# Where VectorE takes the skip and dB in the first two groups with a second phase

## The reference

```python
xz = x @ W_in                                   # 256 -> 2 * 512
x_proj, z = jnp.split(xz, 2, axis=-1)
x_conv = silu(depthwise_conv4(x_proj) + conv_b)  # 4 taps along the sequence
ssm = x_conv @ W_xproj                          # 512 -> 1 + 16 + 16
delta, Bm, Cm = softplus(ssm[..., 0]), ssm[..., 1:17], ssm[..., 17:]
h_mean = einsum('bld,bln->bdn', x_conv, delta[..., None] * Bm) / L
y = einsum('bdn,bln->bld', h_mean, Cm) + D * x_conv
x = layernorm(x + (y * silu(z)) @ W_out)
xq = fp4(x)
h = silu(xq @ fp4(w_gate).T) * (xq @ fp4(w_up).T)
out = layernorm(x + fp4(h) @ fp4(w_down).T)
```

## Time and profile before

| | us |
|---|---|
| median of 3 runs | 1895.02 |
| lowest and highest | 1894.50, 1896.96 |
| the profiled execution | 1894.42 |
| its span | 1892.6 |
| TensorE busy | 1790.6 (95%) |
| VectorE busy | 1625.0 (86%) |
| ScalarE busy | 1269.6 (67%) |
| GpSimd busy | 1120.1 (59%) |

### The profile page before, as it was taken

The page is one execution under the profiler, slowest core; times in us unless marked ns, Lnnn a source line. Parts: engine busy times, 40 slices in busy tenths (PEclk is TensorE's granted clock), DMA queues, the critical chain, the costliest instruction groups (busy, mean ns, idle before and its releaser), DMA issues. The chain is left out here.

```text
span 1892.6 us, 34609 instructions
## 1 busy us (share of the span) xinstructions
PE 1790.6 (95%) x10180; PEld 1545.5 (82%) x10180; DVE 1625.0 (86%) x3697; ACT 1269.6 (67%) x2617; POOL 1120.1 (59%) x1847
## 2 busy tenths in 40 slices
PE   6887999999999999999999999999999999899986
PEld 5666788888888888888888888888888888777775
DVE  6745899899988989999998999899999988888885
ACT  6676677677767777677776777667776776544543
POOL 3334566666656666666666666566666665555453
PEclk9898999999999999999999999999999999999998
DMA  5224232333333233333323333333333333122200
GB/s 175 89 106 159 95 113 94 101 115 114 105 98 109 98 115 104 107 109 108 110 96 106 104 115 104 106 110 97 110 107 106 107 101 106 51 84 68 84 23 17
DMA packets 120312, 190.62 MB, mean 101 GB/s; under 512 B 15040, under 2 KB 49728, under 8 KB 120128
## 3 DMA queue, kind: packets, MB, share of 16 engines
q1 hardware_dynamic: 120128, 188.42, 29.8%
HBM read 104.48 MB, written 83.89 MB: 100 GB/s over the span
## 5 line engine op out<-in xcount | busy, mean ns | idle before, releaser
L572 PE MATMUL pgu<-wgu_hi,xqT 128*128 128x512 f32 (+1 forms) x1536 | 415.2, 379 | 16.6 <-issue 15.4
L572 PEld LDWEIGHTS pgu<-wgu_hi,xqT 128*128 128x128 f32 x1536 | 278.5, 188 | 66.6 <-issue 18.8
L572 PE MATMUL pd<-wd_hi,hqT 128*128 128x256 f32 x1536 | 287.6, 287 | 6.0 <-DVE scratch L1302 2.6
L572 PEld LDWEIGHTS pd<-wd_hi,hqT 128*128 128x128 f32 x1536 | 240.7, 193 | 11.1 <-issue 5.7
L572 PE MATMUL pgu<-wgu_lo,xqT 128*128 128x512 f32 (+1 forms) x768 | 226.6, 376 | 0.0
L1163 DVE SCALAR_TENSOR_TENSOR acc<-xps,cw,acc 128x512 f32<-128x512 f32 x256 | 198.4, 775 | 22.7 <-POOL acc L478 18.0
L1078 DVE SCALAR_TENSOR_TENSOR scratch<-scratch 128x256 f32<-128x256 f32 (+2 forms) x258 | 173.2, 671 | 41.6 <-ACT scratch L957 40.5
L653 PE MATMUL pd<-wout,g 128*128 128x256 f32 x864 | 204.4, 380 | 0.0
L439 POOL TENSOR_SCALAR rs<-ssq 128x1 f32<-128x1 f32 x256 | 79.2, 309 | 201.8 <-issue 187.6
L855 ACT ACTIVATE scratch<-scratch,sum 128x256 f32<-128x256 f32 x256 | 130.0, 508 | 93.3 <-DVE scratch L1248 83.3
L686 PEld LDWEIGHTS pc<-wxp,xcs 128*128 128x128 f32 x1024 | 132.0, 194 | 66.0 <-issue 37.2
(11 more groups left out here) (160 smaller groups left out, 4594.6 us busy)
## 6 DMA issues: line engine op xcount, KB each, us to landing
sz_hbm<-szs SPq DMA_DIRECT2D x128, 256.0 KB, 2.0
xc_hbm<-xcs SPq DMA_DIRECT2D x128, 256.0 KB, 2.0
early<-xc_hbm SPq DMA_DIRECT2D x128, 256.0 KB, 2.7
early<-sz_hbm SPq DMA_DIRECT2D x128, 256.0 KB, 3.0
xin<-in_x_t_dram SPq DMA_DIRECT2D x32, 512.0 KB, 4.7
xres<-in_L_attn_x_dram SPq DMA_DIRECT2D x128, 128.0 KB, 2.4
out_dram<-scratch SPq DMA_DIRECT2D x128, 128.0 KB, 1.7
early<-in_L_attn_W_in_dram SPq DMA_DIRECT2D x2, 512.0 KB, 4.7
```

Source lines behind the costliest of these rows:

```text
L572: mm = pe.matmul(bank, lhsT, rhs, start=(m == 0), stop=(m == len(pairs) - 1))
```

## The change

In groups 5 and 6 alone VectorE's order is changed; nothing is added or removed, and the other engines' orders stay.

- In group 5 (`g_ <= LAG`) `skip()` goes from behind the taps, and in the fourth step from behind two splits of the input, to the front of the step. In its second step dB (`scaled_b()`) goes from behind the rests and codes of the weights to directly behind the taps.
- In group 6 (`g_ == LAG + 1`) `skip()` goes from behind the codes of x, the taps, the rounding and the product of h to the front of the step. From group 7 on it stays where it was.

```diff
                     if g_ <= LAG:
+                        if p2:
+                            skip()
                         tap(1)
                         tap(2)
...
-                        if p2:
-                            skip()
+                        if j == 1 and g_ == LAG:
+                            scaled_b()
                         weight_rests(u)
                         weight_codes(u)
                         if j == 1 and 2 <= g_ < LAG:
                             add_state(g_ - 1)
                         if j == 1 and g_ == LAG:
-                            scaled_b()
                             add_state(g_)
...
                     if exists(tz):
                         ffn_sum()
+                    if g_ == LAG + 1:
+                        skip()
                     if exists(tx):
                         x_codes()
...
-                    if p2:
+                    if p2 and g_ > LAG + 1:
                         skip()
```

## The result

The changed kernel takes 1901.18 us (median of 21 runs, 1897.95 to 1903.23) against 1895.08 (21 runs, 1890.64 to 1898.61): a ratio of 1.0032, with a 95% interval of 1.0026 to 1.0038. It is slower by 6.1 us; the forecast was 7.7 (1902.7, in a range of 1897.5 to 1906.5). The profiled execution took 1901.56, its span is 1899.8, 7.2 longer than before. The page's part 1, to be set beside the earlier trace rows: no engine works appreciably longer, TensorE even 3.3 us less, so the time is idle time.

A forecast was written before the change was run, and what follows sets the result against it. TensorE was taken as the bound, busy 95% of the span. Steps 20 to 25 gave -2.4, steps 26 and 27 +7.7, the clock +2.4: +7.7 us on the 1895.02 median, 1902.7, range 1897.5 to 1906.5.

The forecast's parts named there:

- Step 20: Group 5: y was ready anyway, so skip first puts the taps and the projection behind them 0.7 us later.
- Step 21: Group 5: taps regain 0.6 us beside GpSimd, weight rest goes behind dB; TensorE's partial state starts 0.3 us earlier.
- Step 22: Group 5: the taps wait for y too, so the projection starts at 167.0, not 165.61: 1.4 us later.
- (a): Rival: the 1.2 GHz spells of steps 21 to 24 vanish, step 26 at -6.0, sum +4.1, 1899 us; chance 0.18.
- Step 23: Group 5: the SiLU, no longer the skip, releases the projection; it starts at 173.7 us, +0.5.
- Steps 24 and 25: Group 6: input product +1.0 or -0.4, TensorE's 2.58 us wait for the skip goes; step 26 starts 1.8 to 3.0 earlier.
- Steps 26 and 27: Group 6: skip first makes VectorE wait for y, delaying x's codes and gate product: +4.1 and +3.6, together +7.7 us.
- the 2.4: Clock term: new TensorE pauses around step 27 bring 1.2 GHz spells, costing 0 to 4.8 us; +2.4 taken.
- The steady part: From about 198 us on: TensorE is full, so any delay or gain arriving there remains at the end.
- (b): Rival, faster: the wait for y in steps 26 and 27 is taken up; 1889 to 1893 us, chance 0.05.
- (c): Rival: losses partly absorbed or the clock stays up throughout; 1896 to 1898.8 us, chance 0.12.
- (d): Rival: both new pauses cost a long 1.2 GHz spell; +10.7 us, 1905.7, chance 0.10.

The follow-up runs named there:

- g6_26_27: Skip moved to the front in steps 26 and 27 alone, against the kernel before: 1905.83 us, ratio 1.0054.
- g5_24_25: The changed kernel with the skip back in its old place in steps 26 and 27; against the kernel before: 1894.46 us, ratio 0.9988.
- g6_26: Skip moved to the front in step 26 alone, against the kernel before: 1900.21 us, ratio 1.0028.
- best1: Skip first in steps 23 and 25, dB directly behind the skip in step 21, against the kernel before: 1889.39 us, ratio 0.9967.
- g5_25: Skip first in steps 20 to 23 and 25, dB behind the taps in step 21, against the kernel before: 1892.25 us, ratio 0.9980.
- g5_25_y: Skip first in steps 20 to 23 and 25, dB moved, y before the gate product in 26 and 27; against the kernel before: 1892.96 us, 0.9979.
- s23: Skip moved to the front in step 23 alone, against the kernel before: 1894.93 us, ratio 0.9997.
- g5_only: Group 5 of the change alone (skip first in steps 20 to 23, dB moved), against the kernel before: 1891.76 us, ratio 0.9979.
- warm: Changed kernel plus eight unread filler products before step 27's gate product; against the kernel before: 1899.53 us, ratio 1.0018.
- y_first: Changed kernel with TensorE making y before the gate product in steps 26 and 27; against the kernel before: 1892.84 us, ratio 0.9984.
- y_only: Kernel before with y before the gate product in steps 26 and 27, no skip moved: 1895.37 us, ratio 0.9996 to the kernel before.
- g6_24_25: Skip moved to the front in steps 24 and 25 alone, against the kernel before: 1895.27 us, ratio 1.0003.

## Why the prediction was right

**Steps 20 to 23.** *Step 20* as forecast: the projection at 148.57 against 147.68, less the 0.28 by which y of step 20 was later anyway, +0.6 (forecast +0.7). *Step 21*: partial state at 155.68 against 155.53, so -0.1 (forecast -0.3). Its taps beside GpSimd took 1.57 and not 2.17 us, with the skip put under GpSimd's product; that is the stretch which the walk took away, and the rule of the Trainium skill ("SBUF — State Buffer", section "SBUF: two separate sides") agrees with it. In step 23 the taps took 1.53 against 2.42, but there GpSimd's product had ended at 169.29, before the skip began at 169.56: VectorE had waited 1.18 us for y, which the walk didn't have. The skip took 740 to 749 ns in these places. *Step 22* came out otherwise: the projection at 164.75 and not 167.0, because TensorE ran at full clock there and y was ready 0.28 us after VectorE. That is 0.9 us earlier than before (165.61) where the forecast, and its list of signs, had 1.4 later, and it is a part of rival (a). The wait for y is there, as is a pause of TensorE (1.59 us for the SiLU), but it is small. *Step 23*: 172.47, forecast 173.7.

**Steps 24 and 25.** VectorE waits 3.34 us for y in step 24; the input product of step 25 starts at 185.87 (-0.4; forecast +1.0 or -0.4). That the -0.4 comes out is luck: it stood for no slow stretch in step 24, and there is one (the input product of step 24 takes 1.19 us at its start, as before); TensorE only came in earlier, since step 23 was 0.7 early and not 0.5 late. The wait for the skip in step 25 is gone, and step 26 begins at 197.38, that is -1.9 (forecast -1.8 to -3.0). In the trace this term was well sized, in the runs it is less clear: the changed kernel less g6_26_27 gives 6.1 - 10.2 = -4.1, group 5 alone is -4.0, and g5_24_25, which is the change up to step 25 and nothing else, is -2.3, while I had taken -2.4. The intervals are 2 us and more to each side, so whether the 1.6 us between the forecast of +7.7 and the +6.1 lie in this term can't be decided. What it left out is clear from the traces below: it kept the clock in group 5 at 1.2 GHz from 157 to 162 us as before; I had put the other case apart as rival (a), all or nothing, at -6.0.

**Steps 26 and 27.** +4.4 (forecast +4.1) and +5.9, of which 3.6 and part of the 2.4 were forecast. Here all pieces are in the trace: skip behind y, codes at 203.76, gate product released by the rests, 3.79 us of pause (forecast 3.5), 209 to 216 us at 1.2 GHz, 2.68 before the projection (forecast 2.8). Alone they cost 10.2 us; the terms of the sum give 10.1. The clock's share can be read from the rows: from the gate product of step 27 to its y 7.34 us against 5.88 before, from the z product to the down projection (L572 into pd) 2.29 against 1.47, together 2.3. The 2.4 was the middle between 0 and 4.8, so that it fits so well is in part luck.

**The steady part.** 8.40 us late at step 28 and 8.19 at step 33: it absorbs nothing. Further on the distance moves by about 0.6 us with single slow stretches, as said above.

**Rivals.** (b), faster, fell with the wait of 3.79 and with g6_26. (c) fell too: nothing was absorbed and slow stretches came; its own sum doesn't hold together either, since 5.3 us with no slow stretch would be 1900.3 and not 1896 to 1898.8. (d) was not reached: of the two new pauses one had a stretch of 6.8 us with it, the other one of 3.4. (a) was half right: the stretch behind step 21 went, but the changed kernel has three of 3.4 us, from about 165, 175 and 185 us.

**The gain of group 5.** The medians alone don't say which part of group 5 brings its 4 us: step 23 alone gave nothing that can be told, group 5 with four moved skips 0.9979, best1 with one of these, dB and step 25 0.9967, and g5_25 shows step 25 adding nothing to group 5. Laid side by side, the 14 traces say more. From y of step 20 to y of step 22 the time goes by how much of it TensorE spends at 1.2 GHz:

| at 1.2 GHz between the two | us from y to y | traces |
|---|---|---|
| none | 16.34 to 16.48 | changed, g5_24_25, g5_25, g5_25_y; s23 |
| about 3.4 | 17.02 to 17.91 | g5_only, warm, y_first, best1 |
| 6.9 to 7.9 | 19.19 to 19.70 | before, g6_26_27, g6_26 |
| 10.2 | 20.36 and 20.47 | y_only, g6_24_25 |

The eight kernels with dB moved are the first four and the next four; TensorE's pause for dB is 1.43 to 2.81 us in them. The six with the old order wait 3.10 to 3.15 us, and five of them have 6.9 us or more at 1.2 GHz; only s23 has none. The order itself brings nothing here, since s23 with the old one takes 16.48. So the gain in these two steps is that of the clock, 2.4 us in the mean of the eight against the six. Steps 22 to 25 give a part of it back: y of step 20 to y of step 25 takes 40.92 to 41.50 us in g5_only, g5_25 and g5_25_y, and 43.01 to 44.11 in before, g6_26, g6_26_27 and y_only.

**What stays open.** Each of these is one execution of its kernel, and s23 shows that the old order can come without the stretch as well; how often it does isn't measured. That the shorter pause for dB is the reason, and not another part of the new order, fits best1, where steps 20 and 22 are as before, but best1 without dB wasn't run.

## What to carry to other kernels

Moving an instruction to the front of an engine's order can be free only where its input is ready when the engine gets there: look up in the producer's order what stands ahead of that input, step by step, since one group may have two orders (here the gate product comes in from the third step on). Take each step's move by itself; the same edit took away a wait of 2.58 us in step 25, most of which came back before step 27, and cost 5 us in step 26. A kernel whose main engine is full behind the edited part carries every microsecond to its end, with either sign.

## What the runs showed of the hardware

- TensorE's slow stretches at 1.2 GHz lasted 3.4 or 6.8 us in the parts looked at, now and then 10.2. Many came with or shortly after a pause, but a pause doesn't decide it: that of 3.10 us in step 21 was followed by one before, that of 3.11 in s23 by none, one of 1.42 us in g5_only (projection of step 20) by one of 3.4 us, and in the changed kernel the one of step 27 began within 0.3 us of TensorE's stopping. Over steps 20 and 21 (y to y) no such stretch meant 16.4 us and 10.2 us of it 20.4. The steady part has single ones of 3.4 us, mostly about 219 us apart, and in some executions one or two of them are missing. The times of one and the same kernel before lay between 1890.35 and 1899.24 us.
- The skip, which reads PSUM and SBUF, kept its 0.73 to 0.75 us in all 112 places of all kernels, under a GpSimd product as well; the taps, with both tensors in SBUF, were stretched from 1.53 to 2.17 and 2.42 us beside it before. In the changed kernel they took 1.57 us with the skip under that product, and 1.53 in step 23, where the product had ended before.
